# One kernel, two edits: order of paired semaphore waits, and more idle products on TensorE during the fill

## The reference

```python
x = x + layernorm(attn(layernorm(x)))
x = x + layernorm(ffn(layernorm(x)))

def attn(x):                      # per head, D = 8
    q, k = exp(x @ Wq.T + bq), exp(x @ Wk.T + bk);  v = x @ Wv.T + bv
    kv = cumsum(k[..., :, None] * v[..., None, :], axis=1);  k1 = cumsum(k, axis=1)
    return (einsum(q, kv) / sum(q * k1)) @ Wo.T + bo

def ffn(x):
    logits = rms_norm(x) @ rms_norm(slots).T          # 256 x 512
    h = gelu((softmax over tokens).T @ xn @ w1) @ w2  # 512 slots
    return softmax over slots @ h
```

## Time and profile before

| | before |
|---|---|
| median of three runs | 589.01 us |
| the profiled execution: its own time | 587.3 us |
| its span, first to last instruction | 585.6 us |
| mean granted TensorE clock | 0.985 |
| busy share PE, DVE, ACT, POOL | 95%, 84%, 79%, 80% |
| TensorE waiting for DVE's att, before 33.41 us | 3.64 us |
| TensorE waiting for DVE's xn, before 43.88 us | 3.12 us |
| TensorE busy between 100 and 200 us | 100.00 us |

### The profile page before, as it was taken

One profiled execution on the slowest core, in us unless ns is written; L12 is line 12 of the kernel. 1 busy time (PEld: TensorE's weight loads), 2 busy tenths in 40 slices (PEclk: granted clock), 3 DMA queues, 4 the chain that ended last, 5 costly groups with the idle time before them and its releaser, 6 DMA issues.

```text
span 585.6 us, 10630 instructions
## 1 busy us (share of the span) xinstructions
PE 557.3 (95%) x3774; PEld 489.4 (84%) x3774; DVE 493.9 (84%) x922; ACT 464.9 (79%) x1244; POOL 471.2 (80%) x462
## 2 busy tenths in 40 slices
PE   7936999999999999999999999999999999999986
PEld 7925888888889988888889888888889888888775
DVE  4688889999999898999998999999999999888530
ACT  3137888888889888888889888888889888888763
POOL 4778888898889888898889888998899888984200
PEclk9968999999999999999999999999999999999999
DMA  4000000000100000100000000000000000010000
GB/s 114 12 20 18 10 19 11 20 27 28 28 28 28 20 19 18 28 28 28 27 28 21 27 20 19 27 28 28 28 28 19 27 18 21 19 36 10 11 10 18
DMA packets 16825, 14.29 MB, mean 24 GB/s; under 512 B 2850, under 2 KB 16644, under 8 KB 16772
## 3 DMA queue, kind: packets, MB, share of 16 engines
q1 hardware_dynamic: 14708, 12.76, 7.2%
q10 hardware_dynamic: 2064, 0.86, 0.6%
HBM read 5.25 MB, written 4.19 MB: 16 GB/s over the span
## 4 chain that ended last, share of the span: by engine, by line
PE 89%; DVE 5%; ACT 2%; issue 2%; POOL 1%; POOLq 0%; DVEq 0%
PE banks L1028 17%; PE banks L892 10%; PE banks L1019 10%; PE banks L894 10%; PE banks L893 10%; PE banks L1041 9%; PE banks L999 5%; PE banks L873 3%; PE banks L973 3%; PE banks L974 3%; PE banks L955 2%; PE banks L1008 2%; PE banks L916 1%; PE banks L944 1%; PE banks L981 1%
## 5 line engine op out<-in xcount | busy, mean ns | idle before, releaser
L1028 PE MATMUL banks<-w_c,hid 128*128 128x128 f32 x1024 | 124.7, 275 | 1.4 <-ACT hid L501 1.4
L1028 PEld LDWEIGHTS banks<-w_c,hid 128*128 128x128 f32 x1024 | 121.0, 192 | 2.2 <-ACT hid L501 2.2
L316 POOL TENSOR_TENSOR kv_lo<-kv,kv_hi 128x1152 fp32r<-128x1152 f32 x31 | 81.6, 2633 | 19.5 <-ACT kv_hi L476 19.4
L1302 DVE TENSOR_TENSOR prod<-banks,E 128x768 f32<-128x768 f32 x96 | 85.8, 948 | 3.5 <-PE banks L974 3.5
L1316 DVE TENSOR_REDUCE banks<-prod 128x288 f32<-128x2304 f32 x32 | 81.6, 2549 | 0.0
L375 POOL TENSOR_TENSOR kv<-kv,kv_prev 128x1024 f32<-128x1024 f32 x31 | 74.4, 2400 | 2.2
L1041 PEld LDWEIGHTS banks<-proc,comb 128*128 128x128 f32 x512 | 62.1, 191 | 15.8 <-issue 14.5
L501 ACT ACTIVATE hid<-banks 128x512 f32<-128x512 f32 x128 | 70.7, 617 | 2.5 <-PE banks L894 2.0
L211 POOL TENSOR_TENSOR kv<-E 128x1024 f32<-128x1024 f32 x32 | 68.7, 2147 | 3.0 <-ACT E L476 2.8
L211 POOL TENSOR_TENSOR kv_prev<-prev 128x1024 f32<-128x1024 f32 x31 | 66.4, 2142 | 0.0
L1019 PE MATMUL banks<-disp,xn 128*128 128x512 f32 x128 | 62.6, 611 | 1.9 <-ACT disp L476 1.6
(11 more groups left out here) (140 smaller groups left out, 1552.7 us busy)
## 6 DMA issues: line engine op xcount, KB each, us to landing
X<-in_L_attn_x_dram SPq DMA_DIRECT2D x32, 128.0 KB, 2.1
out_dram<-res SPq DMA_DIRECT2D x32, 128.0 KB, 1.9
prev<-E SPq DMA_DIRECT2D x32, 112.0 KB, 2.1
w_in<-in_L_ffn_w_dram ACTq DMA_DIRECT2D x2, 256.0 KB, 4.7
prev<-E SPq DMA_DIRECT2D x32, 15.0 KB, 2.0
se_in<-n_L_ffn_slot_embeds_dram ACTq DMA_DIRECT2D x1, 256.0 KB, 4.2
w_in<-in_L_attn_Wq_dram SPq DMA_DIRECT2D x1, 64.0 KB, 2.4
w_in<-in_L_attn_Wk_dram SPq DMA_DIRECT2D x1, 64.0 KB, 2.2
```

What stands on the lines that cost most here:

```text
L316: pool.tensor_tensor(kv_lo[:, :], kv[:, :], kv_hi[:, :].bitcast(F32), ALU.subtract)\
L1028: last = pe.matmul(PR[:, j, :], hid[:, f, j * P:(j + 1) * P], w2_c[:, f, :], start=(f == 0), stop=(f == FJ - 1))
L1302: dve.tensor_tensor(prod[u][:, :, d0 * DIM:d1 * DIM].rearrange("p c (d f) -> p c d f", d=g), CU[k].rearrange("p (o d f) -> p o d f", o=1, ...
```

## The change

Two edits. `spin` takes the PSUM bank as an argument, and the fill gets more of these products: 214 instead of 75, with new ones in eight places, in banks 4, 5, 6 and 7. And at each place with two waits the order of the two is turned round, on TensorE in nine functions and on VectorE in three.

```diff
-            def spin(count):
+            def spin(count, bank):
                 for _ in range(count):
-                    pe.matmul(banks[:, 6, 0:P], ident[:, :], ident[:, :], start=True, stop=True)
+                    pe.matmul(banks[:, bank, 0:P], ident[:, :], ident[:, :], start=True, stop=True)
...
             def x_transpose(n):
+                after(pe, disp_ready[0], n - 4)
                 pe.wait_ge(xh_ready, n + 1)
                 if n == 1:
                     after(pe, v_copied, n - 1)
-                after(pe, disp_ready[0], n - 4)
...
             def logits(n):
+                after(pe, gelu_ready[1], n - 1)
                 pe.wait_ge(xnT_lo_ready, n + 1)
-                after(pe, gelu_ready[1], n - 1)
...
             def gather_slots(n):
+                pe.wait_ge(disp_ready[1], n + 1)
                 after(pe, x1_ready, n + 1)
-                pe.wait_ge(disp_ready[1], n + 1)
...
             def first_steps():
                 x_transpose(0)
-                spin(12)
+                spin(12, 6)
                 project(0, 0)
-                spin(1)
+                spin(1, 6)
                 project(0, 1)
-                spin(4)
+                spin(7, 6)
                 x_transpose(1)
-                spin(4)
+                spin(7, 6)
                 project(1, 0)
                 project(1, 1)
                 wo_transpose()
-                spin(40)
+                spin(71, 6)
                 cumulate(0, 2)
                 cumulate(0, 0)
                 cumulate(0, 1)
                 x_transpose(2)
-                spin(8)
+                spin(14, 6)
                 slot_transpose()
                 project(2, 0)
                 project(2, 1)
+                spin(30, 4)
                 att_transpose(0)
+                spin(12, 4)
                 attention_out(0)
+                spin(7, 4)
                 cumulate(1, 2)
...
                 xn_transpose(0)
+                spin(21, 5)
                 logits(0)
                 att_transpose(1)
                 project(3, 0)
                 project(3, 1)
+                spin(11, 5)
                 part_transpose(0)
                 attention_out(1)
+                spin(7, 5)
                 subtract_max(0)
...
                 gather_slots(0)
+                spin(5, 4)
                 xn_transpose(1)
+                spin(3, 4)
                 hidden(0, 0)
```

More of the change, by code:

```diff
@@ L870, in _ @@
         def _(pe):
-            def spin(count):
+            def spin(count, bank):
                 for _ in range(count):
-                    pe.matmul(banks[:, 6, 0:P], ident[:, :], ident[:, :], start=True, stop=True)
+                    pe.matmul(banks[:, bank, 0:P], ident[:, :], ident[:, :], start=True, stop=True)
             pe.wait_ge(s_const, 7)
-            spin(6)
+            spin(6, 7)
             pe.wait_ge(s_wu, 3)
@@ L930, in project @@
                 if c == 0:
+                    pe.wait_ge(xT_lo_ready, n + 1)
                     after(pe, gelu_ready[3], n - 4)
-                    pe.wait_ge(xT_lo_ready, n + 1)
                 elif c == 1:
@@ L948, in attention_out @@
             def attention_out(n):
+                pe.wait_ge(attT_ready, n + 1)
                 if n == 0:
                     pe.wait_ge(s_b_rows, 1)
-                pe.wait_ge(attT_ready, n + 1)
                 pe.matmul(YO, ones_r[:, :], b_rows[:, :, :].rearrange("p c d -> p (c d)"),
@@ L963, in cumulate @@
                 elif k == 1:
+                    after(pe, res_ready, n - 4)
                     if n == 2:
                         pe.wait_ge(kv_lo_ready, n + 1)
-                    after(pe, res_ready, n - 4)
                 elif k == 2:
+                    pe.wait_ge(kv_lo_ready, n + 1)
                     if n in (0, 1):
                         after(pe, v_copied, n + 1)
-                    pe.wait_ge(kv_lo_ready, n + 1)
                 d0, d1 = UNITS[k]
@@ L977, in xn_transpose @@
             def xn_transpose(n):
+                after(pe, comb_ready[1], n - 1)
                 pe.wait_ge(xn_ready, n + 1)
-                after(pe, comb_ready[1], n - 1)
                 for c in range(NC):
@@ L1003, in subtract_max @@
             def subtract_max(n):
+                pe.wait_ge(disp_exp, n + 1)
                 pe.wait_ge(tok_ready, n + 1)
-                pe.wait_ge(disp_exp, n + 1)
                 for g in range(2):
@@ L1033, in mixture @@
             def mixture(n):
-                if n in (30, 31):
-                    after(pe, res_ready, n - 1)
                 after(pe, prod_ready[1], n + 3)
@@ L1038, in mixture @@
                     pe.wait_ge(proc_ready, n + 1)
+                if n in (30, 31):
+                    after(pe, res_ready, n - 1)
                 for c in range(NC):
@@ L1321, in attention @@
             def attention(n):
+                dve.wait_ge(summed, n + 1)
                 dve.wait_ge(own_ready, n + 1)
-                dve.wait_ge(summed, n + 1)
                 dve.tensor_tensor(ND[:, 1, :, :], ND[:, 1, :, :], own[n % 2][:, :, :], ALU.add)\
@@ L1334, in first_residual @@
             def first_residual(n):
+                dve.wait_ge(y_rstd, n + 1)
                 after(dve, res_ready, n - 3)
-                dve.wait_ge(y_rstd, n + 1)
                 for c in range(NC):
@@ L1387, in second_residual @@
             def second_residual(n):
+                dve.wait_ge(o_rstd, n + 1)
                 loaded(dve, stored, n - 2)
-                dve.wait_ge(o_rstd, n + 1)
                 for c in range(NC):
```

## The result

The changed kernel takes 598.75 us (median of four runs, 598.14 to 599.33), against 589.03 for the kernel before (four runs, 588.77 to 589.17). The ratio is 1.0169 [1.0157, 1.0182]: it is slower by 9.7 us. The profiled execution took 599.3 us, with a span of 597.5 and a granted clock of 0.997. Of the later runs of the kernel before, one in the slow state took 1433 us and counts in no ratio.

What follows compares the result with a forecast made beforehand. TensorE was taken as the bound, 89% of the chain. The profiled 587.3 + 12.6 for products - 4.8 for the order of waits = 595.1; 1.7 to the median gives 596.8, said as 597, range 593 to 602.3.

Steps and rivals of the forecast that it cites:

- the products: Fill on TensorE: 139 more idle products make hidden(0, 0) 12.6 us later, a delay carried to the end.
- the order of waits: Steady gather_slots and logits: a late wait written first saves about 0.08 us each, 4.8 us in all with the last mixture.
- Price of a product, and the first cumulative sum: Fill, before cumulate(0, 2): 0.2213 us per product, 31 more are pure delay; the start moves by 7.65 us to 32.2.
- The walk down the fill: Fill on TensorE, place by place: each start's delay after added products and covered waiting, ending at hidden(0, 0), 12.6 us late.
- The clock: Fill: TensorE stays at full clock, giving back 2.2 us already in the walk; a fall at 54 us costs 1.4 more.
- My 1.7 from the profile to the median: Whole kernel: the runs' median is 1.7 us above the profiled execution's 587.3, so this is added to the forecast.
- another chain of the step takes over: Steady step: lower bound of the exchange's gain, 0, if another chain takes over the 0.17 us saved.
- its first rival: Steady step: order brings nothing, another chain such as VectorE's through store and xnT_lo holds 16.5 us; 601.6 us, chance 0.18.
- ruled a new wait out: After the fill: other engines are late by 11 to 12.2 us, less than TensorE, so no new wait arises.
- costed VectorE's and four of TensorE's exchanges at nothing: project, subtract_max, x_transpose, xn_transpose have no gap between matmuls; TensorE does not wait for VectorE's three places: no gain.

Runs made afterwards that it cites:

- e4: Kernel before with one number changed: 71 idle products instead of 40 ahead of cumulate(0, 2); 597.68 us, ratio 1.0145.
- e2: Kernel before with only the changed kernel's 214 idle products, waits in their old order; 599.62 us, ratio 1.0179.
- e10: Changed kernel with SyncE issuing the store ahead of the two shift copies; 597.16 us, ratio 1.0139 against the kernel before.
- e7: e5 with the fill's idle products cut or placed to end before their producers, 24 instead of 40 ahead of cumulate(0, 2); 578.32 us, ratio 0.9824.
- e5: e3 with SyncE issuing the store ahead of the two shift copies; 585.12 us, ratio 0.9940 against the kernel before.
- e6: Kernel before with all exchanges of waits on TensorE and none on VectorE, idle products as before; 587.98 us, ratio 0.9988.
- e11: e3 with the waits also exchanged in x_transpose, project and xn_transpose; 585.90 us, ratio 0.9944 against the kernel before.
- e9: e6 with SyncE issuing the store ahead of the two shift copies; 585.99 us, ratio 0.9943 against the kernel before.
- e3: Kernel before with the waits exchanged in gather_slots and logits alone; 585.36 us, ratio 0.9935.
- e8: Kernel before with one number changed: 24 idle products instead of 40 ahead of cumulate(0, 2); 585.98 us, ratio 0.9952.
- e12: e3 with the waits also exchanged in attention_out, cumulate, subtract_max and mixture; 588.85 us, ratio 0.9997 against the kernel before.
- e1: Kernel before with all exchanges of waits, on TensorE and VectorE, and its 75 idle products; 587.78 us, ratio 0.9974.

## Why the prediction was right, and which of its terms were not

The forecast was 597.0 us in 593 to 602.3, slower; measured were 598.75. Its two terms were both too large, the products by 2.1 us and the order of waits by 3.5. They are of opposite sign and partly cancelled, so that 597.0 came within 1.8 us is in part luck.

- **Price of a product, and the first cumulative sum.** Right: e4 changes this number alone, and the sum moves by 6.92 from its first projection (31 x 0.2213 is 6.9). With nothing to hide it, each product ahead of a producer that is ready is delay, carried down the whole fill.
- **The walk down the fill.** Forecast against the changed kernel's rows and, behind the stroke, e2's: cumulate(0, 2) 32.2: 31.10 / 32.16; att_transpose(0) 44.94: 43.76 / 44.81; attention_out(0) 47.82: 46.58 / 47.63; hidden(0, 0) 73.6: 73.66 / 73.14. e2 follows the walk within 0.5 us at each. By the same profiles the 31 products are 6.9 of e2's 12.2 us, and the other 108, which are 23.9 us of products, cost 5.2: the rest of them fell into waits or was paid for by the clock. The changed kernel's profile began its fill 1.0 earlier (its first projection is at 9.47, in the profile of before it is at 10.51), and then lost 1.6 in the clock's dip, so its agreement at the end is partly luck.
- **The clock.** I took it as full all through, and priced a dip at 1.4 us. Both cases occur. The changed kernel's profile has the dip; e2's, after the same idle time, has not:

```profile
53.93 0.44 PE L981 MATMUL banks<-ident,xn 128*128 128x128 f32 x2 [2.66 <-DVE xn L1354]
54.21 4.85 PE L873 MATMUL banks<-ident 128*128 128x128 f32 x42
58.82 0.36 PE L892 MATMUL banks<-xnT_hi,se_hi 128*128 128x256 f32 x1
```

The 21 products take 4.6 us from start to start here and 6.2 in the changed kernel, so the dip costs 1.6 on the path. In whole runs it shows less evenly: of the changed kernel's four, two are at 598.14 and 598.19 with a mean clock of 1.0 and two at 599.3 with 0.997 or 0.998; of e10's four, one with 1.0 is at 596.83 and three with 0.996 or 0.997 are at 596.66 to 597.51. The Trainium skill (TensorE: Matmul & The Clock Gate, section "Why this matters for your kernels") advises against idle stretches of TensorE between bursts of matmuls. The runs agree with it only with a condition: the clock's return paid in e7, where the products end before the producer, and could not pay for the added products in the changed kernel, where the 71 end 11 us after it (kv_lo is complete at 20.09, the sum starts at 31.10).
- **The fill in the median: -2.** In the profiles hidden(0, 0) is 12.7 and 12.2 late, but e2's median is only 10.5 above before. The reason is in before, not in the change: its profiled execution, at 587.3, is 1.7 under its median, and e2's is at its median. Of the 46 runs of before beside the experiments, ten have a mean clock of 0.985 and take 588.0 to 588.6 us (means of the three batches), and 31 have 0.979 to 0.981, with means of 588.9 to 589.6. The profile that I had is of the first kind, and shorter than any of the ten; the kind accounts for 0.7 to 1.1 of the 1.7. Profiles of the second kind with the fill of before, e5's, e6's and e11's, have a second stretch of half clock around 54 to 58 us and the first gather at 58.8 to 59.1 instead of 57.6. (e9's has this stretch too, at a mean of 0.985, so the mean alone does not tell.) With the added products e2's profile has no such dip. My 1.7 from the profile to the median carried the difference over as if the changed kernel had it too.
- **The order of waits: the failed size, -4.8, measured -1.3.** The mechanism is right: gap by gap the time is 0.08 us shorter at both places. Two things were missing. The step is 0.113 shorter and not 0.166, and that in 27 steps, since the last three take the same 47.7 us in both: about 3.05 in the profiles without disturbed steps (e5, e7), 3.8 in e3's median. I had counted 31 gathers and 26 logits. And waits for the store take 2.5 of the 3.8 back: SyncE issues the store behind the two shift copies, VectorE needs its landing just when it lands, and a step that is disturbed there is 0.4 to 1.5 us longer. The prediction named "another chain of the step takes over" as its bound, and its first rival named VectorE through the store; that chain it was, but not in every step, only in a few. It was not new either: before had 1.9 us of such waits, and e4 and e8, with the old order, had single ones of 2.2 and 2.3 us. The store's part is shown by the store put first, which brings back 2.0 (e9) and 1.6 us (e10), and nothing in e5, where few waits were. I had ruled a new wait out because the other engines are late by less than TensorE, which looked at the fill alone, and had costed VectorE's and four of TensorE's exchanges at nothing; for three of those four (e11) and for VectorE's (e6) no cost can be told, the half with subtract_max cost about 3 (e12 against e11, in one batch).
- **The sum** of medians: 589.0 + 10.5 - 1.3 = 598.2, and 598.75 measured; the 0.5 is within the intervals.

What stays open: why the half with subtract_max's exchange costs about 3 us. That exchange was not tried by itself, only with three functions that have two waits in some batches alone, and the profiles show no gap that it changes at its own place. Nor was the store put first in the kernel before, so how much of the 1.6 to 2.0 us it would bring without any exchange is not known. The banks of the added products were never varied either.

## What to carry to other kernels

An idle product that keeps TensorE's clock up is worth something only as long as it ends before the producer it waits beside: count them from the producer's time, and leave a little waiting behind each group; past that, each costs its full 0.22 us. When you compare the fill of two profiles, count from a common early instruction, and look first whether the clock fell at the same places in both. Of two waits before one instruction, write the one first that comes late, but only at places where the trace shows a gap behind it; doing it everywhere brought a third of what two places brought, until the store was put first. And when a step becomes shorter, look at what is issued behind a waiting instruction in a DMA queue: a store whose buffer is wanted again belongs ahead of the copies that wait for something else.

## What was not expected of the hardware

- The order of two waits matters at all: TensorE starts 0.14 to 0.15 us after a late producer whose wait is written second, and 0.06 to 0.07 when it is first or alone.
- The clock in a fill differs between executions. After 2.65 and 2.66 us of the same idle time it fell in the changed kernel's profile and not in e2's. With the fill of before, the first gather is at 57.6 to 57.7 us (before, e1, e3) or at 58.5 to 59.1 (e5, e6, e9, e11, e12).
- It goes with the start. With the same twelve products ahead of it the first projection is at 9.4 to 10.7 us, and of these fills those that start at 10.51 to 10.61 have no second stretch of half clock at 54 to 58 us, those at 9.44 to 9.95 have it; e12, at 10.38, has one, which ends at 52 to 53 us and not at 49 to 50. Likewise the dip at 54 us is there in the changed kernel and e10 (9.47, 9.46), and not in e2 (10.51). One profile of each is too few to call this a rule.
- The issue of the same two copies takes 1.43 us in most steps and 2.1 to 2.55 in some, and a store that mostly lands in 1.9 to 2.0 us takes up to 4.1 (e8, e10). No place in the span is common to all.
